# Gate scores with the transposed rows as stationary operand, and most input weight tiles split after the gate stage

## The chip, the cores and the metric

The kernel runs on one core of a Trainium2 chip. The metric is the device time of one execution in microseconds. The kernel before took 2631.4 us (median of three runs, 2630.82 to 2631.78).

## The reference

The input x has 8192 rows of 512. Both branches begin with a layer norm of the rows without scale or shift, `xn`:

```
xn = (x - mean) / sqrt(var + 1e-5)
scores = (tanh(xn @ gate_w.T) + 1) * 0.5          # 8192 x 8
out = x + mixer(xn) + experts(xn, scores)
```

The mixer projects xn by `W_in` (2048 x 512), convolves, scans and projects back. The experts take the 1024 best rows of each of 8 experts by the scores. All three work in full precision: weights and data are split into a high and a low part, and a product is three matmuls (high by high, high by low, low by high), except the gate scores, which are f32 matmuls, since they decide which rows are taken.

## The kernel before

Five instruction streams (SP for DMAs, POOL, DVE, PE, ACT) are written by hand and kept in order by semaphores. The program has three stages. `stage_gate` takes the 8192 rows in NB = 16 blocks of 512 rows; `stage_mixer` takes the same blocks in 16 turns; `stage_experts` follows. This change is in `stage_gate` and in the first turn of `stage_mixer`.

**One block of `stage_gate`.** SP loads the block's rows (1 MB) and stores the transposed rows (1 MB). DVE makes the statistics of a block two ahead (L503, L510) and normalises three of the four row tiles (L515), ACT the fourth (L591); POOL makes the small numbers between them (L438 to L450). PE transposes the block, 16 transposes of 128x128 (L564) into four banks, and ACT copies each bank out (L613) to `g_xnt`. Then PE makes the scores: `gw`, 128x8, is the stationary operand and 512 transposed rows move (L572), four f32 matmuls, so the scores come out as 8x512. ACT copies them to `g_sc_t` (L625), PE turns them back with four small transposes (`turn_scores`, L336) one block later, and ACT takes the tanh (L343). The order on PE is: transposes of b, scores of b-1 turned back, scores of b.

**The input weights.** `W_in` is held as 16 tiles of 128x512 f32. In each of the 16 blocks SP loads one (L362, 256 KB, a ring of four buffers `res`), ACT makes its high part (`w_high`, L586) and POOL its low part (`w_low`, L456). The small weights `W_B` and `W_C` are split the same way in the last blocks (L597 to L602, L473, L476).

**The first turn of `stage_mixer`.** PE runs 16 steps `in_step` (r = 0 to 15) of 12 matmuls each (L1590 to L1592), and step r reads weight tile r. `in_step` 0 waits for all 16 low parts. From step 3 on, `share_b` (L1597, L1598) follows each step and needs `u_l` of three channels earlier. Per channel c, ACT evicts the step twice (L1242, L1244), DVE runs three convolution instructions (L1379), ACT the Silu and the high part (L1250, L1256), DVE the low part (`u_low`, L1385). POOL only copies the three halo columns (L1135, L1142). After channel 7 DVE counts the gates (L1420, L1424), and PE sums the counts in a small f32 matmul of the ones matrix, 128x128, by 128x8 (`tally`, L1649). The output weights are loaded and split later in the turn (L1058, L1218, L1122).

```
def turn_scores(pe, b):
    pe.wait_ge(c_sr, b + 1 + 1)
    ...
for k in range(KD):
    pe.wait_ge(c_tc, b * KD + k + 1 + 1)
    pe.matmul(pst, gw[:, k, :], xnt[i][:, k, :], start=(k == 0), stop=(k == KD - 1))
```

Of the kernel before, what the change touches and what calls it, by code (L numbers as in the profile page):

```python
# [254 lines left out]
def stage_gate(mem, t, gates, ident, w, ends, ew, banks, sums):  # L255
# [16 lines left out]
    sc_t = m.sb("g_sc_t", [E, TB])  # L272
# [3 lines left out]
    pst = banks[6][0:E, :]  # L276
    psc = banks[7][:, 0:J * E]
# [19 lines left out]
    c_sr = m.count("g_sr")  # L297
    c_sc = m.count("g_sc")
# [6 lines left out]
    t_tick = m.tick("g_ttick")  # L305
# [3 lines left out]
    c_first = m.count("g_first")  # L309
    c_x = [m.count(f"g_x_in{i}") for i in range(R)]  # L310
    HALF = J // 2
    ON_DVE = J - 1
    own = len(m.counts.counts)
# [16 lines left out]
    def turn_scores(pe, b):  # L330

        pe.wait_ge(c_sr, b + 1 + 1)
        pe.wait_ge(c_ta, b + 1)
        pe.sem_inc(t_tick, 1)
        for j in range(J):
            last = pe.transpose(psc[:, j * E:(j + 1) * E], sc_t[:, j * P:(j + 1) * P],  # L336
                                ident[0:E, 0:E])
        last.then_inc(c_sc, 1)

    def turn_tanh(act, b):  # L340
        act.wait_ge(c_sc, b + 1 + 1)
        act.wait_ge(c_v, b * 2 + 1)
        act.activation(tanh[:, :], psc, ACT.Tanh).then_inc(c_ta, 1)  # L343
# [8 lines left out]
    def end_scores(pe):  # L352
        turn_scores(pe, NB - 1)

    def end_tanh(act):
        turn_tanh(act, NB - 1)

    def sync(sp):
        def load_raw(b, i, first=False):
            if not first:  # L360
                sp.wait_ge(c_wl, b - R + 1 + 1)
            sp.dma_start(w_raw[i][:, :], t["w_in"][:, bass.ds(b, 1), :].rearrange("p o d -> p (o d)")  # L362
                         ).then_inc(c_raw[i], 16)

# [8 lines left out]
        def group(h, first=False, last=False):  # L373
# [17 lines left out]
        for i in range(R):  # L391
            load_raw(i, i, True)
        group(0, first=True)
        with sp.Fori(1, NG - 2) as h:
            group(h)
        sp.dma_start(staged2[0:S, 0:2, :], t["w_c"]).then_inc(c_win, 16)
        sp.dma_start(staged2[S:P, 0:2, :], t["w_c"]).then_inc(c_win, 16)
        sp.dma_start(staged2[:, 2, :], t["w_b"]).then_inc(c_win, 16)
        group(NG - 2, last=True)
# [3 lines left out]
        sp.dma_start(ends.gamma[:, :], t["ln_g"].to_broadcast([P, D])).then_inc(c_win, 16)  # L403
        sp.dma_start(ends.beta[:, :], t["ln_b"].to_broadcast([P, D])).then_inc(c_win, 16)
        for i in range(R):
            if i < R - 1:
                store_xt(NB - R + i, i)

    def gpsimd(pool):
# [42 lines left out]
        def w_low(b, i):  # L452
            tile = bass.ds(b, 1)
            pool.wait_ge(c_wh, b + 1 + 1)
            pool.sem_inc(p_tick, 1)
            pool.tensor_tensor(w_l[:, tile, :].rearrange("p o d -> p (o d)"), w_raw[i][:, :],  # L456
                               f(w_h[:, tile, :]).rearrange("p o d -> p (o d)"),
                               ALU.subtract).then_inc(c_wl, 1)

        for i in range(R):  # L460
            turn(i, i)
            if i > 0:
                w_low(i - 1, i - 1)
        with pool.Fori(1, NG - 1) as h:
            for i in range(R):
                turn(h * R + i, i)
                w_low(h * R + i - 1, (i - 1) % R)
        for i in range(R):
            turn(NB - R + i, i)
            w_low(NB - R + i - 1, (i - 1) % R)  # L470
        w_low(NB - 1, R - 1)
        pool.wait_ge(c_sh, 2 + 1)
        pool.tensor_tensor(w.wc_lh[0:S, :], staged2[0:S, 0:2, :].rearrange("p a b -> p (a b)"),  # L473
                           f(w.wc_hh[0:S, :]), ALU.subtract).then_inc(c_sl, 1)
# [2376 lines left out]
```

## Time and profile before

| | us |
|---|---|
| median of three runs | 2631.4 |
| the profiled execution, its own time | 2631.34 |
| its span | 2629.4 |
| PE busy | 2600.1 (99%) |
| DVE busy | 2080.6 (79%) |
| ACT busy | 1461.9 (56%) |
| POOL busy | 683.2 (26%) |
| first matmul of the mixer starts at | 107.11 |

Busy shares are means over the whole span; the gate stage is its first 4%. PE is the tensor engine's matmuls, PEld its weight loads, and times in a timeline count from the start of the span. A busy time of a merged row reaches to the end of its last instruction, so rows that follow one another overlap by the pipeline's depth; the distance between two starts is what an instruction costs the stream. One f32 matmul is two records of PE and two of PEld; one f32 transpose is one of each.

### The profile page before, as it was taken

To read this page: it belongs to the slowest core of one execution; us is meant where nothing else is said; L and a number is where in the kernel's file an instruction comes from. 1 tells how busy PE (TensorE), PEld (TensorE's weight loads), DVE (VectorE), ACT (ScalarE), POOL (GpSimd) and SP (SyncE) were. 2 spreads that over 40 slices of the span, in tenths; PEclk is the share of its full clock that TensorE was granted. 3 is DMA by queue.
4 is the path that set the end of the run, shared out by engine and by line. 5 is a ranking of instruction groups with operands and counts; after the bars stand their busy time and mean duration, and the time that the engine had idled before them with its cause. 6 is when DMAs were issued, how large, how long until landed. Compare 5 with 4: busy or idle time off the path is not lost.

```text
span 2629.4 us, 38805 instructions
## 1 busy us (share of the span) xinstructions
PE 2600.1 (99%) x11590; PEld 2107.3 (80%) x11592; DVE 2080.6 (79%) x3582; ACT 1461.9 (56%) x2504; POOL 683.2 (26%) x1006
## 2 busy tenths in 40 slices
PE   8999999999999999999999999999999999999998
PEld 4588888888888888888788888888888888888886
DVE  8778888888888888888877778878788787887754
ACT  5744555555555555555545555565555655556553
POOL 5422222222222222223523214113142231411102
PEclk9999999999999999999999999999999999999999
DMA  9733222233333222235447436364363643636313
GB/s 374 259 128 113 79 89 87 88 104 112 112 113 112 84 93 83 89 102 170 138 137 187 109 116 158 92 157 130 115 158 91 157 130 115 159 91 157 98 55 72
DMA packets 262638, 329.62 MB, mean 125 GB/s; under 512 B 142032, under 2 KB 142160, under 8 KB 258640
## 3 DMA queue, kind: packets, MB, share of 16 engines
q1 hardware_dynamic: 228816, 230.91, 28.1%
q0 software_dynamic: 33664, 96.75, 15.0%
q8 instruction: 81, 1.33, 0.2%
q14 instruction: 77, 0.63, 0.1%
HBM read 259.14 MB, written 68.45 MB: 125 GB/s over the span
## 4 chain that ended last, share of the span: by engine, by line
PE 85%; DVE 9%; issue 3%; ACT 1%; DMA 1%; POOL 0%; SPq 0%; DVEq 0%; POOLq 0%; ACTq 0%
PE ring L1590 9%; PE ring L1591 9%; PE ring L1592 9%; PE po L2570 6%; PE po L2572 6%; PE po L2571 6%; PE pb L2572 4%; PE pb L2571 4%; PE pb L2570 4%; PE po L1628 4%; PE po L1629 4%; PE po L1630 4%; PE pc L2572 2%; PE pc L2570 2%; PE pc L2571 2%
## 5 line engine op out<-in xcount | busy, mean ns | idle before, releaser
L2570 PE MATMUL po<-w2h,hid_h 128*128 128x512 f32 x1024 | 399.2, 390 | 2.1 <-DVE hid_l L2507 1.2
L1590 PE MATMUL ring<-xt_h,w_h 128*128 128x512 f32 x1024 | 400.1, 391 | 0.1
L1591 PE MATMUL ring<-xt_l,w_h 128*128 128x512 f32 x1024 | 398.6, 389 | 0.0
L2571 PE MATMUL po<-w2l,hid_h 128*128 128x512 f32 x1024 | 398.4, 389 | 0.0
L1592 PE MATMUL ring<-xt_h,w_l 128*128 128x512 f32 x1024 | 398.4, 389 | 0.0
L1379 DVE SCALAR_TENSOR_TENSOR u<-xin,cw,u 128x512 f32<-128x512 f32 x384 | 288.5, 751 | 73.5 <-issue 44.7
L2047 POOL DMA_INDIRECT out_dram<-res,idx_c x64 | 109.0, 1703 | 488.1 <-DVE res L2417 477.1
L2570 PEld LDWEIGHTS po<-w2h,hid_h 128*128 128x128 f32 x1024 | 192.2, 188 | 44.9 <-DVE hid_l L2407 3.8
L1590 PEld LDWEIGHTS ring<-xt_h,w_h 128*128 128x128 f32 x1024 | 192.2, 188 | 41.0 <-DVE xt_l L543 0.9
L1592 PEld LDWEIGHTS ring<-xt_h,w_l 128*128 128x128 f32 x1024 | 192.2, 188 | 40.1
L2571 PEld LDWEIGHTS po<-w2l,hid_h 128*128 128x128 f32 x1024 | 192.2, 188 | 39.9
L1591 PEld LDWEIGHTS ring<-xt_l,w_h 128*128 128x128 f32 x1024 | 192.2, 188 | 39.4
L2572 PE MATMUL po<-w2h,hid_l 128*128 128x512 f32 x568 | 221.0, 389 | 0.0
L1277 ACT CAST u_h<-u 128x512 fp32r<-128x512 f32 x128 | 79.6, 622 | 226.4 <-DVE u L1410 167.0
L1628 PE MATMUL po<-wo,u_h 128*128 128x512 f32 x512 | 201.2, 393 | 1.2 <-DVE u_l L1414 1.1
L1629 PE MATMUL po<-wo,u_h 128*128 128x512 f32 x512 | 199.6, 390 | 0.0
L1630 PE MATMUL po<-wo,u_l 128*128 128x512 f32 x512 | 199.3, 389 | 0.0
L2401 DVE TENSOR_TENSOR w2l<-w2r,w2h 128x512 fp32r<-128x512 f32 x224 | 152.5, 681 | 36.9 <-ACT w2h L2168 36.9
L1242 ACT COPY xin<-ring 128x512 f32<-128x512 f32 x128 | 75.2, 587 | 167.9 <-PE ring L1592 158.8
L1154 POOL DMA_DIRECT2D wo<-wo_halves x120 | 66.2, 551 | 388.2 <-PE po L1630 313.9
L2168 ACT CAST w2h<-w2r 128x512 fp32r<-128x512 f32 x224 | 137.8, 615 | 29.9 <-PE po L2572 29.6
L2407 DVE TENSOR_TENSOR hid_l<-hid_whole,hid_h 128x512 fp32r<-128x512 f32 x112 | 77.1, 689 | 79.2 <-ACT hid_h L2194 77.5
(299 smaller groups left out, 6234.0 us busy)
## 6 DMA issues: line engine op xcount, KB each, us to landing
w2r<-fc_in SPq DMA_DIRECT2D x256, 256.0 KB
wo<-wo_halves POOLq DMA_DIRECT2D x120, 512.0 KB, 4.4
w1r<-fc_in SPq DMA_DIRECT2D x144, 256.0 KB
x_tail<-x_in SPq DMA_DIRECT2D x64, 256.0 KB, 2.8
out_dram<-res SPq DMA_DIRECT2D x64, 256.0 KB, 2.0
g_x<-x_in SPq DMA_DIRECT2D x15, 1024.0 KB, 9.3
xt_rows<-g_xnt SPq DMA_DIRECT2D x15, 1024.0 KB, 10.9
rows<-xt_rows SPq DMA_DIRECT2D x15, 1024.0 KB, 6.1
```

What stands on the lines that cost most here:

```text
L1379: dve.scalar_tensor_tensor(out=u[:, c, :], in0=x_[:, 3 - q:3 - q + TB], scalar=w.cw[:, c, 3 - q:4 - q], in1=u[:, c, :], op0=ALU.mult, op1= ...
L1590: pe.matmul(ring[r % 2][:, :], w_h[:, r, q], xt_h[:, k, :], start=(k == 0), stop=False)
L1591: pe.matmul(ring[r % 2][:, :], w_h[:, r, q], xt_l[:, k, :], start=False, stop=False)
L1592: last = pe.matmul(ring[r % 2][:, :], w_l[:, r, q], xt_h[:, k, :], start=False, stop=(k == KD - 1))
L1628: pe.matmul(po[j][:, :], y_h[c % 2][:, r], wo[:, c % WO, 0, :], start=(c == 0), stop=False)
L1629: pe.matmul(po[j][:, :], y_h[c % 2][:, r], wo[:, c % WO, 1, :], start=False, stop=False)
L1630: last = pe.matmul(po[j][:, :], y_l[c % 2][:, r], wo[:, c % WO, 0, :], start=False, stop=(c == NC_ - 1))
L2168: act.copy(w2h[x % 4][:, :], w2r[:, x % 8, :]).then_inc(c_wh, 1)
L2401: dve.tensor_tensor(w2l[x % 4][:, :], w2r[:, x % 8, :], f(w2h[x % 4][:, :]), ALU.subtract).then_inc(c_wl, 1)
L2570: pe.matmul(dst, ah, bh, start=start, stop=False, skip_group_check=more)
L2571: pe.matmul(dst, ah, bl, start=False, stop=False, skip_group_check=more)
L2572: return pe.matmul(dst, al, bh, start=False, stop=stop, skip_group_check=more)
```

## The change

The gate matmul is turned round. The transposed rows, 128x128 at a time, become the stationary operand and `gw`, 128x8, moves: 16 matmuls per block in the place of 4, whose result is already 128 rows by 8. The four transposes back (L336), the copy to `g_sc_t` (L625) and their semaphores go, and the scores of alternate blocks lie in two banks. After the gate matmuls of each block PE runs eight transposes of `ident` into an otherwise idle bank; nobody reads them.

Of the input weight tiles, 0 to 3 are still loaded and split at the start of the stage. In the middle blocks none is loaded or split. Tiles 4 to 7 are loaded after the last rows; 4 and 5 are split within the stage and the high parts of 6 and 7 at its end, and everything else (the low parts of 6 and 7, tiles 8 to 15, the low part of `W_B`, both parts of `W_C`) is split by ACT and POOL within the first turn of the mixer. PE now waits for the low part of tile r at step r.

```diff
@@ tensor, one block @@
-                if not (first and i == 0):
-                    turn_scores(pe, b - 1)
-                pe.wait_ge(c_sr, b + 1)
+                if not (first and i < 2):
+                    pe.wait_ge(c_ta, b - 1 + 1)
                 for k in range(KD):
                     pe.wait_ge(c_tc, b * KD + k + 1 + 1)
-                    pe.matmul(pst, gw[:, k, :], xnt[i][:, k, :], start=(k == 0),
-                              stop=(k == KD - 1)).then_inc(c_se, 1)
+                    for j in range(J):
+                        last = pe.matmul(psc[i % 2][:, j * E:(j + 1) * E], xnt[i][:, k, j * P:(j + 1) * P],
+                                         gw[:, k, :], start=(k == 0 and j == 0),
+                                         stop=(k == KD - 1 and j == J - 1))
+                    last.then_inc(c_se, 1)
+                for x in range(WARM):
+                    pe.transpose(spare[:, x % J * P:(x % J + 1) * P], ident[:, :], ident[:, :])
@@ sync @@
                 load_x(NB - R + i if last else b + R, i)
                 store_xt(b, i)
-                load_raw(NB - R + i if last else b + R, i)
...
+        for n in range(R, 2 * R):
+            load_raw(sp, n)
@@ gpsimd, middle blocks @@
                 turn(h * R + i, i)
-                w_low(h * R + i - 1, (i - 1) % R)
@@ mixer: gpsimd, first turn @@
+        in_low(pool, 6)
+        in_low(pool, 7)
+        b_low(pool)
         for c in range(NC_):
             halo_out(0, c)
             if c + 2 < NC_:
                 halo_in(0, c + 2, True)
+            if c % 2 == 1:
+                in_low(pool, 8 + c // 2)
+        in_low(pool, 12)
+        c_low(pool)
+        for n in range(13, NW):
+            in_low(pool, n)
@@ mixer: scalar, first turn @@
+                if first_turn and c % 2 == 1:
+                    in_high(act, 8 + c // 2)
             in_g(b, 0)
             u_pair(b, NC_ - 1)
+            if first_turn:
+                in_high(act, 12)
             in_g(b, 1)
+            if first_turn:
+                c_high(act)
+                in_high(act, 13)
@@ mixer: tensor, in_step @@
-                if type(b) is int and b == 0:
-                    pe.wait_ge(sums.c_in_low, NW + 1)
+            if type(b) is int and b == 0:
+                pe.wait_ge(sums.c_in_low, r + 1 + 1)
```

Here is PE's stream in the first group of `stage_gate`, one block, before: 16 transposes, the scores of the block ahead turned back, and the four gate matmuls (`po`, `pb`, `pc` are banks).

```order
L564 MATMUL po<-ident,g_x 128x128 x16
L336 MATMUL pc<-ident,g_sc_t 128x8 x4
L572 MATMUL pb<-g_xnt,g_gw 8x512 x4
L564 MATMUL po<-ident,g_x 128x128 x16
L336 MATMUL pc<-ident,g_sc_t 128x8 x4
L572 MATMUL pb<-g_xnt,g_gw 8x512 x4
```

The same place in the change:

```order
L561 MATMUL po<-ident,g_x 128x128 x16
L569 MATMUL pc<-g_gw,g_xnt 128x8 x16
L574 MATMUL ring<-ident 128x128 x8
L561 MATMUL po<-ident,g_x 128x128 x16
L569 MATMUL pb<-g_gw,g_xnt 128x8 x16
L574 MATMUL ring<-ident 128x128 x8
```

A block's 24 instructions have become 40, and every one of the 16 gate matmuls loads 128 columns where each of the four loaded 8.

POOL's stream in the first turn of the mixer before, from the last of the small constants through the channels to the output weights:

```order
L1142 COPY halo<-xin 128x3
L1135 COPY xin<-halo 128x3
L1142 COPY halo<-xin 128x3
L1135 COPY xin<-halo 128x3
L1142 COPY halo<-xin 128x3 x2
L1122 TENSOR_TENSOR wo<-res,wo 128x512 x8
```

And in the change:

```order
L344 TENSOR_TENSOR w_l<-res,w_h 128x512 x2
L352 TENSOR_TENSOR wb<-g_staged_53,wb 128x8x64
L1132 COPY halo<-xin 128x3
L1125 COPY xin<-halo 128x3
L1132 COPY halo<-xin 128x3
L1125 COPY xin<-halo 128x3
L344 TENSOR_TENSOR w_l<-res,w_h 128x512
L1132 COPY halo<-xin 128x3
L1125 COPY xin<-halo 128x3
```

Every second channel is followed by the low part of one weight tile, which was made in the gate stage before; three more low parts stand ahead of the first halo copy.

## Rows read from the trace of the kernel before

**Rows 1.** Windows of two stretches of the gate stage, busy us of each engine.
```profile
core 0: us, PE busy (x) PEld busy (x) DVE busy (x) ACT busy (x) POOL busy (x), PEclk, DMA share, GB/s
20.00:40.00 20.00, 20.00 (x91) 8.59 (x90) 18.70 (x47) 13.51 (x28) 12.77 (x28) 1.00 1.03 412
40.00:60.00 20.00, 19.60 (x100) 9.56 (x99) 18.65 (x44) 13.19 (x27) 12.59 (x27) 1.00 1.03 413
```

**Rows 2.** Timeline of PE, gate stage: start us, us, what, idle before.
```profile
17.64 1.97 PE L564 MATMUL po<-ident,g_x 128*128 128x128 f32 x16 [1.15 <-ACT g_x L591]
...
34.96 1.96 PE L564 MATMUL po<-ident,g_x 128*128 128x128 f32 x16
36.86 0.41 PE L336 MATMUL pc<-ident,g_sc_t 8*128 8x8 f32 x4
37.20 3.60 PE L572 MATMUL pb<-g_xnt,g_gw 128*8 128x512 f32 x8
40.73 1.97 PE L564 MATMUL po<-ident,g_x 128*128 128x128 f32 x16
```

**Rows 3.** Timeline of DVE, same stretch.
```profile
40.82 2.47 DVE L503 BATCH_NORM_STATS2 g_stats<-g_x 128x6 f32<-128x512 f32 x4 [0.21 <-DMA g_x<-x_in]
...
43.98 2.40 DVE L515 TENSOR_SCALAR g_x<-g_x,g_mv,g_rstd 128x512 f32<-128x512 f32 x3
46.41 2.47 DVE L503 BATCH_NORM_STATS2 g_stats<-g_x 128x6 f32<-128x512 f32 x4
```

**Rows 4.** Line L515 in 44.4 to 45.2 us, then timeline of POOL beside it.
```profile
L515 DVE TENSOR_SCALAR g_x<-g_x,g_mv,g_rstd x2: 541/1016/1491, 44.0 to 44.4; 128x512 f32<-128x512 f32 x2
...
44.35 1.29 POOL L456 TENSOR_TENSOR w_l<-res,w_h 128x512 f32 x1 [1.60 <-ACT w_h L586]
```

**Rows 5.** Timeline of PE around a tally in the first turn.
```profile
166.11 0.39 PE L1629 MATMUL po<-wo,u_h 128*128 128x512 f32 x1
166.34 0.39 PE L1630 MATMUL po<-wo,u_l 128*128 128x512 f32 x1
166.57 0.28 PE L1649 MATMUL pb<-narrow,l_both 128*128 128x8 f32 x2
166.71 0.48 PE L1615 MATMUL pc<-h_hh,wc_hh 128*128 128x512 f32 x1
167.02 0.40 PE L1616 MATMUL pc<-h_hl,wc_lh 128*128 128x512 f32 x1
```

**Rows 6.** Timeline of PE's weight loads at the same place.
```profile
166.34 0.41 PEld L1649 LDWEIGHTS pb<-narrow,l_both 128*128 128x128 f32 x2
166.68 0.19 PEld L1615 LDWEIGHTS pc<-h_hh,wc_hh 128*128 128x128 f32 x1
166.79 0.19 PEld L1616 LDWEIGHTS pc<-h_hl,wc_lh 128*128 128x128 f32 x1
```

**Rows 7.** Timeline of PE from the first transpose on.
```profile
8.47 1.94 PE L556 MATMUL po<-ident,g_x 128*128 128x128 f32 x8 [8.47 <-DVE g_x L495]
10.21 1.91 PE L564 MATMUL po<-ident,g_x 128*128 128x128 f32 x8
12.05 4.44 PE L572 MATMUL pb<-g_xnt,g_gw 128*8 128x512 f32 x8
```

**Rows 8.** Timeline of PE, first turn of the mixer.
```profile
107.11 0.50 PE L1590 MATMUL ring<-xt_h,w_h 128*128 128x512 f32 x1
...
118.69 0.39 PE L1597 MATMUL pb<-u_h,wb 128*128 128x512 f32 x1
...
121.86 0.39 PE L1597 MATMUL pb<-u_h,wb 128*128 128x512 f32 x1
...
138.76 0.39 PE L1649 MATMUL pc<-narrow,l_both 128*128 128x8 f32 x2 [0.42 <-DVE narrow L1424]
```

**Rows 9.** Timeline of DVE, first turn of the mixer.
```profile
118.57 2.33 DVE L1379 SCALAR_TENSOR_TENSOR u<-xin,cw,u 128x512 f32<-128x512 f32 x3 [0.52 <-ACT u L1244]
120.81 0.68 DVE L1385 TENSOR_TENSOR u_l<-u,u_h 128x512 fp32r<-128x512 f32 x1
...
136.69 0.69 DVE L1385 TENSOR_TENSOR u_l<-u,u_h 128x512 fp32r<-128x512 f32 x1 [0.75 <-ACT u_h L1256]
137.30 0.69 DVE L1420 TENSOR_TENSOR l_gt<-gates,narrow 128x512 bf16<-128x512 f32 x1
```

**Rows 10.** Timelines of POOL and DVE where two weight tiles meet a count.
```profile
154.66 2.98 POOL L1122 TENSOR_TENSOR wo<-res,wo 128x512 fp32r<-128x512 f32 x2 [5.15 <-ACT wo L1218]
...
154.70 1.79 DVE L1420 TENSOR_TENSOR l_gt<-gates,narrow 128x512 bf16<-128x512 f32 x1
```

More of the change, by code:

```diff
@@ L275, in stage_gate @@
     pt = banks[0:KD]
-    pst = banks[6][0:E, :]
-    psc = banks[7][:, 0:J * E]
+    spare = banks[4]
+    psc = [banks[6 + i][:, 0:J * E] for i in range(2)]
     w_raw = ends.res
@@ L350, in end_values @@
         gate_values(dve, NB - 1)
-    def end_scores(pe):
-        turn_scores(pe, NB - 1)
     def end_tanh(act):
-        turn_tanh(act, NB - 1)
+        scores_tanh(act, NB - 1, R - 1)
     def sync(sp):
[L359 to L363, printed above, removed]
         def load_x(b, i):
@@ L371, in store_xt, with group @@
             sp.dma_start(xs_v[at(b)], xnt[i][:, :, :]).then_inc(c_xs[i], 16)
-        def group(h, first=False, last=False):
+        def group(h, last=False):
             for i in range(R):
@@ L402, in sync @@
         sp.dma_start(w.dp[:, :], t["d_param"]).then_inc(c_win, 16)
[L403 to L407, printed above, removed]
+        for i in range(R - 1):
+            store_xt(NB - R + i, i)
+        sp.dma_start(ends.gamma[:, :], t["ln_g"].to_broadcast([P, D])).then_inc(c_first, 16)
+        sp.dma_start(ends.beta[:, :], t["ln_b"].to_broadcast([P, D])).then_inc(c_first, 16)
     def gpsimd(pool):
@@ L581, in scalar @@
     def scalar(act):
-        def w_high(b, h, i):
-            act.wait_ge(c_raw[i], h * 16 + 16 + 1)
-            tile = bass.ds(b, 1)
-            act.copy(w_h[:, tile, :].rearrange("p o d -> p (o d)"), w_raw[i][:, :]).then_inc(c_wh, 1)
         def normalise(b, i):
@@ L606, in group @@
                 b = h * R + i
-                if last and i == R - 1:
-                    w_high(b, h, i)
                 if not first:
@@ L616, in group @@
                 if not (first and i == 0):
-                    turn_tanh(act, b - 1)
+                    scores_tanh(act, b - 1, (i - 1) % R)
+                if first:
+                    w_high(act, i)
                 if not (last and i == R - 1):
-                    w_high(b, h, i)
                     normalise(b + 1, (i + 1) % R)
-                if last and i < 3:
-                    small_high(i)
-                act.wait_ge(c_se, (b + 1) * KD + 1)
-                act.wait_ge(c_sc, b + 1)
-                act.copy(sc_t[:, :], pst).then_inc(c_sr, 1)
+                if last and i in (1, 2):
+                    w_high(act, R + i - 1)
         group(0, first=True)
@@ L630, in scalar @@
         group(NG - 1, last=True)
[L632 removed]
+        for n in (R + 2, R + 3):
+            w_high(act, n)
+        b_high(act)
+    return sync, gpsimd, vector, tensor, scalar, end_store, end_values, end_tanh, \
+        load_raw, w_high, w_low, b_low, c_high, c_low
 class Experts:
@@ L1088, in sync @@
         load_rows(1)
-        sp.wait_ge(sums.c_in_low, NW + 1)
-        for c in range(4):
-            load_raw(c)
+        for n in range(8, 12):
+            in_raw(sp, n)
         end_store(sp)
+        for n in range(12, NW):
+            in_raw(sp, n)
         for j in range(J):
             ends.load_x(sp, 0, j, True)
+        for c in range(4):
+            sp.wait_ge(sums.c_in_low, NW - 4 + c + 1 + 1)
+            load_raw(c)
         for c in range(4):
```

111 lines of the change are left out of this document (55 added, 56 removed).

## The prediction

> **What bounds the kernel now.** I read the windows of the gate stage first, since the change lies there and in the turn behind it. PE is busy 20.00 of 20 us, DVE 18.70, and the DMA engines are full at 412 GB/s [rows 1]. Three resources are thus near their limit, and the timelines tell which one sets the pace. On PE a block is 34.96 to 40.73, 5.77 us, with no idle time: 1.90 us for 16 transposes, 0.34 for the four that turn the scores back, 3.53 for the four gate matmuls [rows 2]. So PE paces the steady blocks. DVE's own round, from one L503 to the next, is 46.41 - 40.82 = 5.59 us [rows 3]. The DMA moves 2 MB of rows and 0.25 MB of weights a block, 2.36 million bytes, which at 412 GB/s is 5.73 us. All three would need to fall for the stage to gain much.
>
> The mixer's first matmul starts at 107.11 with nothing idle before it [rows 8], 89.5 us after block 1 started at 17.64 [rows 2], for 15 blocks: 5.96 us a block, so small stalls on DVE and the loads add some 2.8 us to 15 x 5.77. In the mixer PE is the bound: whatever ends the gate stage later ends the kernel later by as much.
>
> **The gate matmuls, turned round.** Removed are four matmuls with 8 columns stationary and 512 moving, 3.53 us a block. Added are 16 f32 matmuls with 128 columns stationary and 8 moving. The trace has the very same form: the tally, 128x128 by 128x8 in f32, two records each. A 512-column matmul costs 166.34 - 166.11 = 0.23 us. The tally starts at 166.57, and L1616 at 167.02; take off one 512-column matmul (L1615, 0.23) and 0.22 us are left for the tally's two records [rows 5]. The weight loads say why: L1615's load starts at 166.68 and the next at 166.79, when the matmul before has taken its weights, so one load of 128 columns takes 0.11 us, and eight moving columns don't hide it [rows 6]. A block's gate is then 16 x 2 x 0.11 = 3.52 us: **the turn brings nothing on PE**. The matmuls' work fell 16 times over, but the weight loads took its place.
>
> The page TensorE: Matmul & The Clock Gate of the Trainium skill has a table (Back-to-back issue gap) by which a matmul of 1 to 64 columns follows the last after about 60 cycles, 25 ns; by that alone the gate would be an estimated 32 x 0.025 = 0.8 us. The rows here show 0.11 us, so I keep 3.52.
>
> Removed too are the four transposes back, 0.34 us a block, and the waits for ACT's copy, of which PE showed none.
>
> **The eight spare transposes.** A transpose of 128x128 costs (1.97 us less the last one's own 0.28)/15 = 0.11 us [rows 2]; eight are 0.88. They stand in PE's stream behind the gate matmuls and ahead of the next block's transposes, and cover no wait if PE sets the pace. A block is now 1.90 + 3.52 + 0.88 + 0.10 (one change of form, as now) = **6.40 us**, against 5.77.
>
> **DVE, POOL, ACT and the DMA in the gate stage.** One L515 of three takes 1491 ns where its neighbour takes 541, and it started at 44.4, with POOL's low part at 44.35 for 1.29 us [rows 4]. Without that low part DVE's round falls by 0.95 to 4.64 us. The DMA loses the 0.25 MB: 2.10 million bytes at 412 GB/s are 5.09 us. ACT loses 0.65 (the high part) and 0.57 (the copy). All of these fall below PE's 6.40, and so are worth only the 2.8 us of small stalls. This is where the expected gain goes: off the path.
>
> **When the mixer starts.** Block 0 starts at 8.47 as before. Its gate begins at 12.05; while PE is slow (the first 16 transposes take 3.58 us [rows 7], against 1.90 later [rows 2]) a record costs 0.22. The gate of block 0 ends by about 16.5 and the spare ones by 17.4, still ahead of block 1 at 17.64, which waits for ACT's L591 behind a weight tile's load [rows 2]; neither is touched. Then 15 blocks: 17.64 + 15 x 6.40 = 113.6, **6.5 us later** than 107.11. The low part of the last rows is ready before that. In the first turn the last scores' four transposes go: -0.3.
>
> **The first turn of the mixer.** ACT gets 8 high parts (0.62 each) and the two of W_C (1.07 each); POOL gets 10 low parts of input tiles at 1.27 to 1.29, W_B's and W_C's (2.35). A low part needs its tile in time: step 6 comes 17 us after the mixer's start, and POOL makes tile 6 in the first 4; tiles 8 to 15 each have several us. SP issues them behind one 1 MB load, and none of the loads is late by this count. The price lies elsewhere, in DVE. A two-input DVE instruction beside POOL's low parts took 1.79 us where it takes 0.69 [rows 9, 10]: 1.10 us a meeting. DVE has little room: u_low of channel 1 ends at 121.49 and PE reads it at 121.86 [rows 8, 9], and PE already waits 0.42 for DVE at the first tally [rows 8], where the only idle time just ahead on DVE is 0.75 [rows 9]. Five low parts (tiles 8 to 12) fall ahead of that tally: between 0 (all land in gaps) and 5 x 1.10 = 5.5 us. ACT's high part of tile 8 also stands between u_h of channel 0 and the eviction of channel 2, and pushes DVE's next convolution by 0.6. I take three meetings in five, 3.2 us, since DVE is near its limit there but has about 0.3 us of slack in each step.
>
> **Sum** against the profiled execution's own 2631.34 us (span 2629.4; the median is 2631.4, the same within its spread): +6.5 - 0.3 + 3.2 = +9.4, **2640.7 us**. With 0 and 5.5 for the first turn, and 6.3 to 6.5 for a block, it is 2636 to 2645. A measurement here can tell 0.2%, 5.3 us, from no change.
>
> **The rivals.**
> 1. *The gate gets cheap.* If the weight loads ran at the pace of the four small transposes, (0.41 - 0.21)/3 = 0.07 us [rows 2], the gate would be 2.2 and PE's block 5.1, level with the DMA's 5.09. The mixer starts at 17.64 + 15 x 5.1 = 94.1, 13.0 earlier; with -0.3 and +3.2, **2621.2 us**. For it: those transposes load 128 columns too. Against it: they are transposes, one record each, and the tally is the same form as the new gate. It decides when a record costs less than about 0.085 us. Chance 0.13.
> 2. *PE runs at its low clock.* PE's first transposes take 0.22 us apiece, those of block 1 0.11: the low level (1.2 GHz) and the high one (2.4), and the rise came while the gate matmuls of block 0 ran, after 3.6 us of transposes alone had not brought it [rows 7]. The granted clock then stays 1.00 [rows 1]. The new stage has transposes, short matmuls and weight loads, and no 512-column matmul. If the clock stays low for the whole stage, a block costs 12.8 and the time is 2640.7 + 15 x 6.4 = **2737 us**; chance 0.12. If it is low for two to eight blocks it is 2653 to 2692; chance 0.14. Against it: PE is never idle. The same page (Part 4: PE-mode transpose) says that transposes don't count as PE-busy and the full clock doesn't engage for them. By that rule the spare transposes would be of no use and this rival is the likely one; the rows of block 0 neither exclude nor show it.
> 3. *The spare transposes and moved tiles do nothing and all costs cancel.* Were the first turn free and a block 6.1 us, it would be 2633; this makes most of the chance of no change.
>
> **How the numbers follow.** My forecast has 0.61, rival 1 0.13, the low clock 0.26. The chance of faster by over 0.2% is rival 1, 0.13. No change gets 0.10, from the low end of my own case, the rest, 0.77, is slower. The range, 2620 to 2680, takes in my case, nearly all of rival 1 and the shorter low-clock cases, and leaves out the stage that is slow throughout. The likeliest case's own range is 2636 to 2645.
>
> **What would show it.** Right: a steady block of 6.3 to 6.5 us on PE without idle time, its gate part 3.5 us, weight loads 0.11 apart; L515 at 541 ns in every block and the DMA below 400 GB/s; the mixer's first matmul near 113.6; PE waiting on DVE in the first turn, with L1379 or L1385 stretched beside POOL's low parts. Wrong: a gate part near 1 or 2 us and PE waiting for DVE or a load in the steady blocks (rival 1), a granted clock of 0.5 or records 0.22 apart past block 0 (rival 2), or PE waiting for a weight tile's low part, which I cost at nothing.

## The result and the profile after

The change takes 2673.45 us (median of 5 runs, 2673.35 to 2675.15), the kernel before 2631.78 beside it (5 runs, 2630.82 to 2633.02): 1.0158 times as long, 95% interval 1.0147 to 1.0169. The profiled execution has an own time of 2673.35 us and a span of 2671.4; its mean granted clock is 0.984, where that of before is 0.999.

From the page of the change, the busy times and the strip of the granted clock:

```profile
PE 2642.0 (99%) x12040; PEld 2197.3 (82%) x12040; DVE 2077.6 (78%) x3582; ACT 1455.5 (54%) x2488; POOL 682.2 (26%) x1006
PEclk7799999999999999999999999999999999999999
```

PE is 99% busy, and in the first two of 40 slices (67 us each) it had 0.7 of its clock. These 134 us lie wholly in the gate stage, which now lasts until 142.90. The windows of the change, two of the stretches of [rows 1] and then the whole stage from block 1 to the mixer:

```profile
core 0: us, PE busy (x) PEld busy (x) DVE busy (x) ACT busy (x) POOL busy (x), PEclk, DMA share, GB/s
20.00:40.00 20.00, 20.00 (x156) 20.00 (x155) 15.00 (x39) 10.19 (x21) 9.97 (x24) 0.84 0.94 310
40.00:60.00 20.00, 20.00 (x126) 20.00 (x126) 10.65 (x33) 6.18 (x12) 4.76 (x14) 0.67 0.82 262
...
18.60:142.90 124.30, 124.28 (x841) 124.30 (x841) 64.91 (x182) 50.36 (x101) 37.28 (x99) 0.73 0.80 259
```

PE has no idle time, and DVE and the DMA have become loose (10.65 of 20 us, 262 GB/s; [rows 1] had 18.65 and 413). But the clock is 0.73 over the stage, where it was 1.00. The timeline of PE shows how that mean comes about, first in block 0, then over a block that is wholly at the high level, then around a later one:

```profile
8.66 1.94 PE L553 MATMUL po<-ident,g_x 128*128 128x128 f32 x8 [8.66 <-DVE g_x L492]
10.40 1.56 PE L561 MATMUL po<-ident,g_x 128*128 128x128 f32 x8
11.79 4.07 PE L569 MATMUL pb<-g_gw,g_xnt 128*128 128x8 f32 x32
...
29.69 3.64 PE L569 MATMUL pb<-g_gw,g_xnt 128*128 128x8 f32 x32
33.18 1.07 PE L574 MATMUL ring<-ident 128*128 128x128 f32 x8
34.09 1.91 PE L561 MATMUL po<-ident,g_x 128*128 128x128 f32 x16
35.84 4.17 PE L569 MATMUL pc<-g_gw,g_xnt 128*128 128x8 f32 x32
...
57.30 1.95 PE L574 MATMUL ring<-ident 128*128 128x128 f32 x8
59.04 3.62 PE L561 MATMUL po<-ident,g_x 128*128 128x128 f32 x16
62.46 3.73 PE L569 MATMUL pb<-g_gw,g_xnt 128*128 128x8 f32 x32
66.04 1.95 PE L574 MATMUL ring<-ident 128*128 128x128 f32 x8
```

From 29.69 to 35.84 the level is high: 3.49 us for the gate's 32 records, 0.91 for the eight spare transposes, 1.75 for the 16 transposes, a block of 6.15 us. From 57.30 on the spare ones take 1.74 and the transposes 3.42, twice as long; the gate after them takes 3.58, the high level's price, and the spare ones at 66.04 are slow again. In 13 of the 15 blocks the 16 transposes take more than at the high level (2.2 to 3.4 us from start to start instead of 1.75); only those at 34.09 and at 109.26 don't. The windows over those two parts say the same:

```profile
57.30:62.40 5.10, 5.10 (x25) 5.10 (x26) 1.32 (x6) 1.73 (x3) 2.02 (x6) 0.50 0.86 302
62.50:66.00 3.50, 3.50 (x33) 3.50 (x33) 2.47 (x7) 1.39 (x3) 0.00 (x0) 0.98 0.45 95
```

So in most blocks the low level (1.2 GHz) lies over the transposes and the high one (2.4) over the gate: **the level mostly rises after PE has done transposes, and mostly falls after PE has done the gate.** It is no rule for every block: it did not fall after the gates at 29.69 and 104.86. The first rise is of this kind too: the first eight transposes take 1.74 us from start to start, the next eight 1.39, so the level rose while they ran. The mixer starts at 142.90 instead of 107.11.

The time splits by the start of block 1, the mixer's first matmul, and channel 0 of the first turn (the first L1627 record, L1615 of before, at 189.50 and 147.98):

| | block 1 starts | 15 blocks | first turn | rest | span |
|---|---|---|---|---|---|
| before | 17.64 | 89.47 | 40.87 | 2481.4 | 2629.4 |
| the change | 18.62 | 124.28 | 46.61 | 2481.9 | 2671.4 |
| difference | +0.98 | +34.81 | +5.74 | +0.5 | +42.0 |

Of the +34.81, the clock is most. At the high level 15 blocks of 6.15 us would be 92.3 us, so about 32 us are the clock's. (By the mean clock alone, 124.3 x 0.73 = 90.7; that is a little low, since at the low level the instructions cost 1.92 times as much, 6.69 against 3.49 us for the gate, and not twice.) The other 2.8 us are two parts of opposite sign: 15 x (6.15 - 5.77) = 5.7 us more work on PE, less the 2.9 us of small stalls of before, which are gone.

The +0.98 ahead of block 1 is a wait of PE for which the profile names no releaser. DVE and POOL of the change show what PE stood for:

```profile
16.10 2.42 DVE L512 TENSOR_SCALAR g_x<-g_x,g_mv,g_rstd 128x512 f32<-128x512 f32 x3
...
16.97 1.27 POOL L344 TENSOR_TENSOR w_l<-res,w_h 128x512 fp32r<-128x512 f32 x1 [1.15 <-ACT w_h L339]
```

The three normalises of block 1 end at 18.52, and PE starts at 18.62. Before, they began at 16.09 and took 1.43, with POOL's low part starting at 17.06, 0.09 later than here. It is the meeting of [rows 4], in the first group, whose low parts the change leaves in place.

In the first turn, PE, DVE and POOL of the change:

```profile
175.09 0.50 PE L1609 MATMUL pb<-u_h,wb 128*128 128x512 f32 x1 [0.40 <-DVE u_l L1396]
...
177.85 0.39 PE L1661 MATMUL pc<-narrow,l_both 128*128 128x8 f32 x2 [2.03 <-DVE narrow L1435]
...
183.72 0.36 PE L1661 MATMUL pc<-narrow,l_both 128*128 128x8 f32 x2 [0.58 <-DVE narrow L1435]
```

```profile
157.92 2.32 DVE L1390 SCALAR_TENSOR_TENSOR u<-xin,cw,u 128x512 f32<-128x512 f32 x3
160.75 3.23 DVE L1390 SCALAR_TENSOR_TENSOR u<-xin,cw,u 128x512 f32<-128x512 f32 x3
...
178.54 3.25 DVE L1442 TENSOR_TENSOR threshold<-threshold,narrow 128x8 f32<-128x8 f32 x1
```

```profile
160.84 1.80 POOL L344 TENSOR_TENSOR w_l<-res,w_h 128x512 fp32r<-128x512 f32 x1
...
178.17 2.37 POOL L361 TENSOR_TENSOR wc_lh<-g_staged,wc_hh 64x1024 fp32r<-64x1024 f32 x1
180.50 1.26 POOL L344 TENSOR_TENSOR w_l<-res,w_h 128x512 fp32r<-128x512 f32 x1
```

DVE's convolution beside a low part takes 3.23 us where the one ahead of it takes 2.32, and the 128x8 threshold takes 3.25: it starts at 178.54, inside POOL's 2.37 us, and ends at 181.79, when POOL's second low part ends. PE's wait ahead of the first tally is 2.03 us where [rows 8] has 0.42. The clock is low at two places of the turn, at its start and after that wait. Windows of both:

```profile
142.90:145.00 2.10, 2.10 (x8) 1.72 (x7) 0.00 (x0) 0.00 (x0) 1.83 (x4) 0.60 0.01 4
...
178.20:182.60 4.40, 4.40 (x14) 3.45 (x14) 4.21 (x5) 1.19 (x2) 3.57 (x3) 0.61 0.46 157
```

### The profile page after: what moved, and what is told of

Its sections match the earlier page's. It is cut to its first block, busy times and chain, and to the rows that moved or that the text cites. A ratio compares the mean times of both kernels' runs of the same rounds, so it can differ in the third digit from the quotient of the medians.

```text
span 2671.4 us, 39640 instructions
## 1 busy us (share of the span) xinstructions
PE 2642.0 (99%) x12040; PEld 2197.3 (82%) x12040; DVE 2077.6 (78%) x3582; ACT 1455.5 (54%) x2488; POOL 682.2 (26%) x1006
## 4 chain that ended last, share of the span: by engine, by line
PE 85%; DVE 10%; issue 2%; ACT 1%; POOL 0%; DVEq 0%; SPq 0%; POOLq 0%; ACTq 0%
PE ring L1602 8%; PE ring L1603 8%; PE ring L1604 8%; PE po L2582 5%; PE po L2583 5%; PE po L2584 5%; PE po L1640 4%; PE po L1641 4%; PE po L1642 4%; PE pb L2584 4%; PE pb L2582 4%; PE pb L2583 4%; PE pc L2583 2%; PE pc L2582 2%; PE pc L2584 2%
## 5 line engine op out<-in xcount | busy, mean ns | idle before, releaser
L1390 DVE SCALAR_TENSOR_TENSOR u<-xin,cw,u 128x512 f32<-128x512 f32 x384 | 291.2, 758 | 75.8 <-issue 44.4
```

Of the source, the lines that this page charges most:

```text
L1390: dve.scalar_tensor_tensor(out=u[:, c, :], in0=x_[:, 3 - q:3 - q + TB], scalar=w.cw[:, c, 3 - q:4 - q], in1=u[:, c, :], op0=ALU.mult, op1= ...
```

## The experiments

My theory after the result: the granted clock, which changes with what PE has just done, is nearly all of the loss in the stage, and POOL's low parts cost the rest in the first turn through DVE. The rivals: that the spare transposes themselves hold the clock down, since they are transposes; that the moved tiles cost the time; and that a different placing of the same work keeps the clock. All ratios are against the kernel before, run on the same chip, with 95% intervals.

### The spare transposes spread between the gate's parts (e1_spread)

```diff
@@ tensor engine of the change, a block
                 for k in range(KD):
                     for j in range(J):
                         last = pe.matmul(psc[i % 2][:, j * E:(j + 1) * E], ...)
+                    for x in range(2):
+                        pe.transpose(spare[:, x * P:(x + 1) * P], ident, ident)
-                for x in range(WARM):
-                    pe.transpose(spare[:, x % J * P:(x % J + 1) * P], ident[:, :], ident[:, :])
```

> The change with its eight spare transposes spread: two behind the four gate matmuls of each k, in the place of eight at the block's end. Same instructions, another order. Theory A (the granted clock follows what PE did just before: transposes raise it, a run of weight loads with 8-column matmuls lets it fall, and the change puts all of the one kind in one run and all of the other in the next): the granted clock stays at 1.00 or near it, a block costs 6.4 us in the place of 8.3, the mixer starts near 114 and the time is 2643 to 2648. Theory B (the stage has too little matmul work for the high level, however it is ordered): the mean clock of the stage stays near 0.73 or falls, 2670 or more.

Measured: 2690.37 us, 1.0223 (1.0206 to 1.0240), 17 us slower than the change with the same instructions. The mixer starts at 155.55, a block is 9.04 us. A window, and a block's transposes on PE:

```profile
80.00:100.00 20.00, 20.00 (x120) 20.00 (x120) 11.81 (x35) 6.20 (x12) 4.13 (x13) 0.62 0.84 255
```

```profile
39.96 3.62 PE L561 MATMUL po<-ident,g_x 128*128 128x128 f32 x16
```

The transposes of the rows are slow again (3.62). Only the order of the same work differs, and the clock is granted less (0.62 here, 0.66 over the stage, where the change has 0.73): where the transposes stand matters, not just their number. Theory A as I had put it failed: it had 2643 to 2648 at a clock near 1.00. Theory B's forecast held, though the order should have made no difference to it.

### No spare transposes (e2_no_spare)

```diff
-    WARM = 8
+    WARM = 0
```

> The change without any spare transposes. Theory A: transposes raise the clock, so with a third fewer of them the level is lower than 0.73 on average, and what is saved in instructions is partly lost; a block costs 7.5 to 10 us, the time is 2660 to 2700. Theory C (transposes do not count for the clock, only matmuls do; the spare ones are a pure cost of 1.75 us a block at the low level): the clock's pattern stays and the time falls by 15 x 1.75, to about 2647.

Measured: 2698.53 us, 1.0228 (1.0190 to 1.0266). The four runs spread from 2679.65 to 2702.64, far more than those of the other kernels; the fastest of them is still slower than every run of the change (at most 2675.15). In the profile, which is of the slowest, the mixer starts at 167.62 and a block is 9.92 us.

```profile
60.00:80.00 20.00, 20.00 (x97) 20.00 (x95) 8.89 (x26) 6.29 (x12) 3.79 (x13) 0.50 0.62 206
```

```profile
42.45 6.83 PE L569 MATMUL pc<-g_gw,g_xnt 128*128 128x8 f32 x32
49.14 3.65 PE L561 MATMUL po<-ident,g_x 128*128 128x128 f32 x16
```

PE is busy 20.00 of 20 us and stays at the low level: the gate takes 6.69 us, 0.209 a record. Over the whole stage the clock is 0.51; it rose once, in one block. The spare transposes thus buy 1.64 us a block (9.92 less 8.28) although they cost at least 0.91 themselves. The rival that they hold the clock down has fallen, and with it theory C's 2647; the measured time and block lie in theory A's ranges.

### The change with the old gate (e3_old_gate), and the turned gate alone (e4_turn_alone)

e3_old_gate keeps the moved tiles and puts back the gate of before, its turn of the scores and ACT's copy:

```diff
-                    for j in range(J):
-                        last = pe.matmul(psc[i % 2][:, j * E:(j + 1) * E], xnt[i][:, k, j * P:(j + 1) * P],
-                                         gw[:, k, :], ...)
+                    pe.matmul(pst, gw[:, k, :], xnt[i][:, k, :], start=(k == 0),
+                              stop=(k == KD - 1)).then_inc(c_se, 1)
-                for x in range(WARM):
-                    pe.transpose(spare[:, x % J * P:(x % J + 1) * P], ident[:, :], ident[:, :])
```

> The gate matmuls of the kernel before (gw stationary, 512 rows moving, scores turned back), with the weight tiles split where the change splits them: the moved tiles alone. By my steps: a steady block on PE stays 5.77 us, the instruction of DVE that took 1491 ns takes 541 in every block, the small stalls shrink, so the mixer starts at 104.3 to 106 (107.1 before); the first turn costs 3 to 6 us more, as in the change: 2631 to 2635. Rival: the first turn's cost came from the clock alone, then it is under 1 us and the time is 2628 to 2630.

e4_turn_alone is the kernel before with the turned gate and the eight spare transposes; all weight tiles are split in the stage as before:

```diff
-                    pe.matmul(pst, gw[:, k, :], xnt[i][:, k, :], start=(k == 0),
-                              stop=(k == KD - 1)).then_inc(c_se, 1)
+                    for j in range(J):
+                        last = pe.matmul(psc[i % 2][:, j * E:(j + 1) * E], xnt[i][:, k, j * P:(j + 1) * P],
+                                         gw[:, k, :], ...)
+                for x in range(2 * J):
+                    pe.transpose(spare[:, x % J * P:(x % J + 1) * P], ident[:, :], ident[:, :])
```

> The turned gate with eight spare transposes at the block's end, with all weight tiles loaded and split in the gate stage as before: the turned gate alone. Theory A: the clock alternates as in the change, a block costs about 8.3 us, the mixer starts near 143; the first turn is that of the kernel before, less 0.3. Time 2666 to 2669, so the moved tiles cost 4 to 6 us. Rival (the moved tiles pay for themselves within the stage): 2673 or more.

Measured: the moved tiles alone 2637.16 us, 1.0016 (1.0006 to 1.0026); the turned gate alone 2671.50, 1.0144 (1.0127 to 1.0161). The turned gate is the loss, with 8.50 us a block and a first turn of 41.73. With the moved tiles alone a block is 5.95 us in the mean, as before, and the turn is 46.45. That mean hides two parts: 14 blocks of 5.77 without a stall, and block 1 with 8.53. Ahead of block 1 PE waits 3.72 us until 18.95: DVE's three normalises meet POOL's low part there too, take 2.38 us and end at 18.85. A low spell follows. So the mixer starts at 108.21, not at the 104.3 to 106 that I expected, and the time is 2 us above my range. PE of e3_old_gate:

```profile
67.84 1.97 PE L578 MATMUL po<-ident,g_x 128*128 128x128 f32 x16
73.61 1.97 PE L578 MATMUL po<-ident,g_x 128*128 128x128 f32 x16
...
143.02 0.39 PE L1677 MATMUL pc<-narrow,l_both 128*128 128x8 f32 x2 [2.03 <-DVE narrow L1451]
```

Its steady block is 5.77 us, [rows 2]'s, at the high level; and the 2.03 us wait at the first tally is there without the turned gate. e4_turn_alone is 2.5 us above the 2666 to 2669 that I gave it: its block 0 ran at the low level to the end, block 1 starts at 20.68 and the mixer at 148.14. Its wait at the first tally is the 0.42 of [rows 8]. The longer wait is followed by a low spell in both kernels that have it: in e3_old_gate it is this window.

```profile
143.20:148.50 5.30, 5.13 (x16) 3.72 (x16) 4.91 (x6) 1.92 (x4) 3.74 (x3) 0.68 0.42 133
```

### Sixteen spare transposes (e5_run16)

```diff
-    WARM = 8
+    WARM = 16
```

> The change with sixteen spare transposes at each block's end in the place of eight. After the first four runs the theory reads (A2): the clock's level follows how much of a stretch of PE's time streams columns; transposes do, the gate's weight loads with 8-column matmuls do not; only an unbroken run of transposes raised it, and spreading them over the gate lost that. Then a longer run raises the level: mean clock of the stage above 0.73. All at the high level a block would be 7.3 us, so 8 to 9 us a block and 2670 to 2690. Rival (the gate's loads pull the level down after every block whatever precedes them): mean clock 0.73 or lower, a block 9.3 or more, 2690 or more.

Measured: 2689.91 us, 1.0221 (1.0192 to 1.0251). The mixer starts at 158.87. The trace has both behaviours in one stage, as windows and PE's timeline show:

```profile
76.50:86.80 10.30, 10.30 (x66) 10.30 (x65) 4.45 (x13) 2.85 (x7) 2.02 (x6) 0.67 0.59 205
86.80:98.00 11.20, 11.20 (x104) 11.20 (x103) 7.47 (x21) 4.57 (x10) 2.31 (x6) 1.00 0.78 229
...
120.00:140.00 20.00, 20.00 (x141) 20.00 (x139) 6.70 (x23) 6.98 (x14) 5.70 (x13) 0.75 0.73 267
```

```profile
86.83 3.64 PE L569 MATMUL pc<-g_gw,g_xnt 128*128 128x8 f32 x32
...
121.93 3.64 PE L569 MATMUL pb<-g_gw,g_xnt 128*128 128x8 f32 x32
...
130.62 4.27 PE L569 MATMUL pc<-g_gw,g_xnt 128*128 128x8 f32 x32
```

From 86.83 to 121.93 five blocks pass at 7.02 us each with the clock at 1.00; then it alternates again. PE did the same sequence throughout and waited for nothing. The alternation isn't tied to one instruction: in the seven blocks up to there the 16 transposes take 2.93, 2.85, 2.76, 2.68, 2.60, 2.52 and 2.45 us, so the rise comes a little earlier in each block, until the level holds; after it they begin at 3.00 and shrink again. Even in the best stretch a block is 7.02 us, more than the 5.96 of before: filler enough to hold the clock for a while costs more than the old gate. Over the stage the clock is 0.77 and a block 9.12 us. That is A2's direction (a clock above 0.73), at the slow end of its forecast: the time is at the edge of its 2670 to 2690, the block just over its 8 to 9.

### Gate matmuls and transposes one by one (e6_pairs), with spare ones between (e7_pairs8, e8_pairs16)

The gate of block b-1 is laid between the transposes of block b. e7_pairs8 adds a spare transpose after every second gate matmul, e8_pairs16 after every one.

```diff
                     last = pe.transpose(...)
+                    if not (first and i == 0):
+                        gate_part((i - 1) % R, k, j)
...
-                for x in range(WARM):
-                    pe.transpose(spare[:, x % J * P:(x % J + 1) * P], ident[:, :], ident[:, :])
```

> The change without spare transposes, and with the gate matmuls of block b-1 placed one by one between the transposes of block b (one transpose, one gate matmul), so that every weight load of the one can run beside the streaming of the other. By the rows: per pair 0.11 (a transpose's columns, beside the gate's first load) + 0.11 (the second load) + 0.05 to 0.06 (the transpose's load) = 0.28 us, 4.5 us a block at the high level, where the DMA or DVE then set about 5.1. Columns stream in some 38% of the time, evenly. If that is enough for the high level: mixer starts near 98, time 2626 to 2630. If not: 9 us a block, 2685 to 2695.

> As e6_pairs, with eight spare transposes a block, one behind every second gate matmul: columns stream in about half of the time, evenly. High level: 5.2 to 5.5 us a block, 2630 to 2634. Low: 10.5 a block, 2705 to 2715. A2 expects this one to be at the high level rather than e6; a theory in which only long unbroken runs of streaming count expects the low level in both.

> As e6_pairs, with a spare transpose behind every gate matmul, sixteen a block: columns stream in about 57% of the time. High level: 5.9 to 6.3 us a block, 2638 to 2645. Low: 12 us a block, 2730.

Measured: 2726.20 us, 1.0359 (1.0329 to 1.0389); 2744.86, 1.0430 (1.0400 to 1.0460); 2771.54, 1.0532 (1.0501 to 1.0562). PE of e6_pairs, and a window of e8_pairs16:

```profile
60.48 0.45 PE L570 MATMUL po<-ident,g_x 128*128 128x128 f32 x1
...
61.01 0.45 PE L570 MATMUL po<-ident,g_x 128*128 128x128 f32 x1
```

```profile
60.00:80.00 20.00, 15.71 (x82) 15.13 (x83) 8.49 (x22) 5.05 (x10) 2.02 (x6) 0.50 0.45 147
```

From one transpose to the next, with a gate matmul between them, are 0.53 us, nearly twice the 0.28 reckoned for the high level, and the granted clock of e8_pairs16 is 0.50: the mixture stays at the low level, and more spare transposes in it only add their own time. The clock column of e6_pairs and e7_pairs8 reads 1.00 over their stage, as it does for the first microseconds of the change, whose transposes are 0.22 apart; I go by the distances, so for these two the low level is inferred. A2 expected e7_pairs8 at the high level, and that failed. All three are also 30 to 40 us above the times that I gave for the low level, in which I had put no waits. The three are therefore not a clean test of mixture alone, since PE now also waits for rows (in e6_pairs 29.6 us in 12 waits; in e8_pairs16 it is busy 15.71 of 20), and idle time may have its own part in the clock.

### A 512-column matmul as filler (e9_matmul_filler)

One f32 matmul of the old gate's form in place of the eight spare transposes; its result is used by nobody.

```diff
-                for x in range(WARM):
-                    pe.transpose(spare[:, x % J * P:(x % J + 1) * P], ident[:, :], ident[:, :])
+                pe.matmul(spare[0:E, :], gw[:, 0, :], xnt[i][:, 0, :], start=True, stop=True)
```

> The change with one f32 matmul of the old form (gw stationary, 512 rows moving, 0.88 us at the high level) at each block's end in the place of the eight spare transposes (0.88 us): the same streaming time in another kind of instruction. A2 (what counts is an unbroken stretch of streaming, whichever instruction does it): the clock alternates as in the change, mean 0.70 to 0.80, 2665 to 2685. Theory C (transposes count for little, matmuls for much): the matmul keeps the level up, mean clock 0.9 or more, a block 6.5 to 7 us, 2645 to 2655.

Measured: 2676.42 us, 1.0166 (1.0145 to 1.0186), and 8.31 us a block. PE's timeline and a window:

```profile
42.52 1.88 PE L573 MATMUL ring<-g_xnt,g_gw 128*8 128x512 f32 x2
44.33 3.54 PE L561 MATMUL po<-ident,g_x 128*128 128x128 f32 x16
47.71 3.81 PE L569 MATMUL pb<-g_gw,g_xnt 128*128 128x8 f32 x32
```

```profile
60.00:100.00 40.00, 40.00 (x232) 32.96 (x231) 19.75 (x62) 15.14 (x30) 11.80 (x31) 0.70 0.78 247
```

The same alternation (slow transposes, fast gate), the same time: 1.8 us of matmul at the low level do for the clock what 1.74 us of transposes do. The stage's clock (0.76) and the time are in A2's ranges, and theory C's are missed: that the filler is a transpose isn't what fails.

### The moved low parts made small (e10_no_low, e11_no_low_again)

Both are e3_old_gate with nearly all of the work of the low parts of tiles 8 to 15 and of `W_C` taken away (those of 6, 7 and `W_B` stay); ACT's high parts, SP's loads and the order stay.

```diff
-        pool.tensor_tensor(w_l[:, n, :], w_raw[n % R][:, :], f(w_h[:, n, :]), ALU.subtract).then_inc(c_wl, 1)
+        w = 8 if n >= 8 else D
+        pool.tensor_tensor(w_l[:, n, 0:w], w_raw[n % R][:, 0:w], f(w_h[:, n, 0:w]), ALU.subtract).then_inc(c_wl, 1)
```

> e3_old_gate, with POOL's low parts of tiles 8 to 15 and of W_C cut to 8 columns each (the rest of these low parts is set to zero in the gate stage, so the low halves of half of the input weights and of W_C are left out of the products); every wait, load and high part stays. It takes away POOL's use of the port that it shares with DVE in the first turn, and nothing else. If the first turn's cost comes from DVE being held by POOL: the convolutions take 2.33 us in every channel, the small threshold instruction (3.26 us in e3) 0.2, PE waits 0.4 or less at the first tally, the clock does not dip, and the first turn is 0 to 1.5 us longer than before in the place of 5.9: 2631 to 2634. If it comes from ACT's added high parts: PE still waits 1.5 us or more at the first tally and the time stays at 2636 to 2638.

Measured: 2636.25 us, 1.0011 (1.0001 to 1.0021), with a first turn of 41.24 us. The gain was eaten up in the stage, where PE waits 2.9 and 4.4 us for rows in the profile, each time followed by a low spell. The 4.4 us were made by my edit: the zeroing of the left-out parts stood on POOL from 30.94 to 35.56, behind a low part, and DVE's three normalises beside them took 7.02 us. The 2.9 us, ahead of block 1, were not: there ACT normalises its row tile behind the first weight tile's high part, and that tile's load came late.

So I ran it again with the zeroing in the last four blocks.

> e10 again, since its zeroing of the left-out low parts stood on POOL ahead of block 4 and held up the stage by some 5 us: here POOL zeroes them (the same parts are left out) in the last four blocks, where it has time. Stage as in e3_old_gate, first turn as in e10 (41.2 us from the mixer's first matmul to chan 0, 46.4 in e3): 2631 to 2633. If the time stays at 2636 or more, the 5 us that e10 saved in the turn are lost again behind it, and the first turn is not the whole cost of the moved tiles.

Measured: 2629.11 us, 0.9990 (0.9981 to 0.9999). The stage is 5.77 us a block, the mixer starts at 104.24, the first turn is 41.23. DVE's convolution and threshold, where the change has 3.23 and 3.25:

```profile
127.60 2.32 DVE L1410 SCALAR_TENSOR_TENSOR u<-xin,cw,u 128x512 f32<-128x512 f32 x3
...
136.95 0.17 DVE L1462 TENSOR_TENSOR threshold<-threshold,narrow 128x8 f32<-128x8 f32 x1
```

POOL's low parts of tiles 8 to 15 and `W_C` alone make the difference of 5.2 us between the first turns of e3_old_gate (46.45) and this one. The high parts and loads that ACT and SP got cost 0.4 at most, against 40.87 of before. And the 2.9 us of small stalls in the stage do go when the tiles leave it: 0.1% is what moving them could give if their low parts were free in the turn. The time is 2 us below the 2631 to 2633 that I expected.

### The low parts in the stage, behind the rows (e12_low_behind_rows)

The kernel before, with POOL's low part kept back until DVE has normalised the block's rows: the collision of [rows 4] goes and nothing moves to the mixer.

```diff
+                pool.wait_ge(c_xn, (b + 1) * ON_DVE + 1 + 1)
```

> The kernel before, unchanged but for one wait: in the gate stage POOL makes the low part of a weight tile only when DVE has normalised its three row tiles of that block, so that the two never ask for the shared port at once. If the collision is what stretches one normalise instruction to 1491 ns: all take 541, DVE's round falls from 5.59 to 4.7, PE's block stays 5.77 without the 2.8 us of small stalls, the mixer starts at 104.3 to 106, 2628.5 to 2630. Rival: POOL, held back, gives its next small numbers too late, and PE waits for DVE in every block: 2633 or more.

Measured: 2631.37 us, 0.9996 (0.9987 to 1.0005): no difference that can be told. DVE and PE of this run:

```profile
45.48 1.45 DVE L521 TENSOR_SCALAR g_x<-g_x,g_mv,g_rstd 128x512 f32<-128x512 f32 x3
```

```profile
17.67 2.99 PE L570 MATMUL po<-ident,g_x 128*128 128x128 f32 x16 [2.19 <-ACT g_x L597]
...
77.61 1.97 PE L570 MATMUL po<-ident,g_x 128*128 128x128 f32 x16 [0.68 <-DVE g_x L521]
```

The three normalises take 1.45 us where [rows 3] has 2.40, and the mixer starts at 106.90, 0.2 earlier than before. Small waits of PE for rows remain and a low spell stands at the start of block 1 (the first 16 transposes take 2.99 us, not 1.97), behind a wait of 2.19 us where before had 1.15. Block 1 thus costs 7.29 us in the place of 5.77, which with 1.0 us of waits for DVE later takes back nearly all that the collisions had cost. Neither of the two expectations came true. No kernel of these runs that computes the whole result is measurably faster than the kernel before.

## Why the prediction was right, and where it was not

The forecast was slower by 9.4 us, 2640.7, in a range of 2620 to 2680. It is slower, and 2673.45 is in the range; but by another case than the one I held likeliest, and 33 us above its figure. The difference is +42 us where +9.4 was forecast. That the range held is owed to its width, drawn for the shorter low-clock cases, and not to the mechanism that I believed in: for my own case it is luck.

**Right: the gate turned round brings nothing on PE.** The forecast was 32 x 0.11 = 3.52 us a block and 6.40 a block; measured at the high level are 3.49 and 6.15 (the change of form of 0.10 doesn't show, and 16 transposes took 1.75 start to start, not 1.90). It seems that the forecast counted the change of form twice, since the 1.90 of [rows 2] runs to the next form's start. PE's work in the stage rose by 5.7 us at the high level, where I had 9.5. The table in the page TensorE: Matmul & The Clock Gate of the Trainium skill, section Back-to-back issue gap, gave the estimate of 0.8 us; the same section says that such a gap leaves the weight loads out and is too short for few columns. With another stationary tile for each matmul the loads are the time here, 0.109 us a record, so the 0.8 was the wrong thing to take from it. Rival 1 (cheap gate) is out.

**Right: DVE, POOL, ACT and the DMA fall off the path.** PE waited for nothing between 20 and 142 us, and in the middle blocks DVE's collision with the low part went. e11_no_low_again gives the price of what went: 2.9 us over the stage, the 2.8 of the prediction.

**Wrong: "the granted clock then stays 1.00", with "PE is never idle" against rival 2.** This is the step that failed, and it is as large as the whole miss, about 32 us; the errors of the other terms nearly cancel. I took idle time to be what the clock answers to. PE was never idle and had 0.73 of the clock; in e2_no_spare it was never idle and had 0.50. Rival 2's second form, the low clock over a part, is what happened, but not as two to eight whole blocks: it is about half of most blocks. Its bound, 2653 to 2692, held the result. I saw that the new stage has no 512-column matmul and still gave rival 2 only 0.26. The rows of before held no stretch with this mix at the high level, so there was nothing to hold the 1.00 on.

**The page's rule against the change did not hold, its conclusion nearly did.** The same page (Part 4: PE-mode transpose) says transposes don't count as PE-busy. In the change's block 0 the level rose while PE had done nothing but transposes (1.74 us for eight, then 1.39). It rises over and over during or right after the spare and the following transposes, and a real matmul as filler did no better (e9_matmul_filler). What lets the level fall is the turned gate: with the old gate and the same transposes it holds (e3_old_gate). Whether its weight loads or its 8-column matmuls do it wasn't told apart. The rise of block 0 of before came during its gate matmuls [rows 7], and I read too much into that; in the change it came a little earlier, on transposes.

**Mis-sized: block 1 and the first turn.** Block 1 starts 0.98 us later, where I had nothing and wrote that "neither is touched". Block 0 itself was in time: its spare transposes begin at 15.71 and end at 17.66, against 17.4 in the forecast. Then PE stands still for 0.96, and the rows of DVE and POOL above show why: DVE's third normalise fell behind POOL's low part. The turn was forecast at +3.2 - 0.3 and came to +5.74. Its place was right (DVE beside POOL's low parts, PE's wait at the first tally), and so was the zero for loads and late low parts. But I counted only what PE waits for: that is 3.01 us less the 0.42 of before, 2.6. On top come two low spells of the clock: at the mixer's start (2.10 us at 0.60: 0.8 lost) and after the 2.03 us wait (4.40 us at 0.61: 1.7 lost). The remaining 0.6 is in small steps.

**By parts.** The turned gate with its spare transposes is +39 alone (e4_turn_alone), the moved tiles +5 alone (e3_old_gate); together they are +42, not +44. The difference of 2 us is within what the intervals leave open, and isn't explained.

## What to carry to other kernels

Before making a matmul "smaller" by turning it round, count weight loads: with a new 128-column stationary tile for every 8 moving columns the loads are the time, and the clock may not be held under them. A stage's length at full clock must be divided by the share of the clock that its own mix of instructions is granted, and a busy PE says nothing about that; look for a stretch of the trace with the same mix, and if there is none, put a good part of the chance on the low level. Work moved off one bound stage into another is paid there by whoever shares a port with it: make sure that the neighbour has slack of the whole length of the moved instructions, several in a row.

## What the runs showed of the hardware

- **PE 100% busy at half its clock.** With transposes and the turned gate only, PE was busy 20.00 of 20 us at a granted clock of 0.50 (e2_no_spare). With eight transposes more a block (the change) it was up for most of each block's gate and down for part or all of the transposes of 13 in 15.
- **The same sequence, two behaviours.** In e5_run16 the clock was 1.00 for five blocks and alternated before and after, with no wait of PE in between; the place of the rise drifted through the blocks until it held. Block 0 differs too: the change and e4_turn_alone run the same sequence on PE there, and the gate takes 3.92 us in the one and 6.68 in the other. What tips it isn't in these runs.
- **Order counts.** The same instructions in another order cost 17 us (e1_spread against the change).
- **A short wait can cost more than itself.** After PE's wait of 2.03 us a low spell cost 1.7 us in the change (4.40 us at 0.61) and in e3_old_gate (5.30 at 0.68); after waits of 0.42 in e4_turn_alone and e11_no_low_again it did not come. In the gate stage too, a low spell stands behind the waits of 2.19 (e12_low_behind_rows), 2.85 and 4.36 (e10_no_low) and 3.72 us (e3_old_gate), and none behind 1.15 (before) and 1.28 (e11_no_low_again). That it's the wait's length that decides is argued from these rows, not shown by changing it alone.
- **A tiny DVE instruction behind two of POOL's.** The 128x8 threshold took 3.25 us beside POOL's low parts and 0.17 without them (e11_no_low_again). The page SBUF — State Buffer of the Trainium skill (section SBUF: two separate sides) says that a DVE instruction with two SBUF inputs and a POOL instruction that reads SBUF shut each other out for the whole instruction; the trace agrees, and adds that DVE's turn came only after POOL's second instruction, since it ended at 181.79 with POOL's at 181.76. In e10_no_low three normalises, 1.43 us without POOL, took 7.02 beside a low part and nine zeroing instructions of POOL in a row.
